# Attention and mixture-of-experts block: the causal mask inside the shift product, the rotation summed by VectorE out of a PSUM bank

## What is computed

```python
h = tok(x, channel_weights)                  # 12x224x224 image: 16x16 patches summed, 12 channels -> 192: 196 tokens
h = concatenate([h, txt], axis=1)            # + 32 text tokens: 228 tokens per batch item, 64 items
xn = norm_scale * layernorm(h) + norm_bias
q, k, v = split(xn @ W_attn + b_attn)        # 12 heads of 16
q, k = rope(q), rope(k)                      # o0 = x0*cos - x1*sin ; o1 = x0*sin + x1*cos
att = softmax([sink, causal(q @ k.T / 4)])[..., 1:]
h = h + (att @ v @ W_proj + b_proj) * rezero
h = h + moe(layernorm(h))                    # 8 experts, top 2, capacity 1.25, RMS norm, SwiGLU of width 512
```

## Time and profile before

| | us |
|---|---|
| median of three runs | 2927.87 (2925.61 to 2928.73) |
| the profiled execution | 2924.14 |
| its span | 2922.3 |
| TensorE busy | 2783.5 (95%) |
| TensorE weight loads busy | 2512.5 (86%) |
| VectorE busy | 2029.5 (69%) |
| GpSimd busy | 2019.7 (69%) |
| ScalarE busy | 1692.1 (58%) |
| mean granted TensorE clock | 0.979 of full |

### The profile page before, as it was taken

How to read it: one execution, slowest core, us unless ns; L and a number is a source line. 1 busy time by engine, 2 the same in 40 slices (tenths; PEclk the granted TensorE clock), 3 DMA queues, 4 the chain that set the end, 5 groups by cost and what they waited for, 6 DMA issues and landing times. The chain is left out here.

```text
span 2922.3 us, 65980 instructions
## 1 busy us (share of the span) xinstructions
PE 2783.5 (95%) x21712; PEld 2512.5 (86%) x21712; DVE 2029.5 (69%) x5657; ACT 1692.1 (58%) x4074; POOL 2019.7 (69%) x2070
## 2 busy tenths in 40 slices
PE   2899999999999999999999977999999999999998
PEld 1788888888888888888888866999999989999997
DVE  3577777777777777777777745767676767676766
ACT  0466666666666666666666644656565656565655
POOL 3578888888888888888888743656565655565665
PEclk8899999999999999999999978999999999999999
DMA  6455544444444444444344223333333333323242
GB/s 187 146 178 176 172 166 170 156 122 123 120 112 108 111 122 122 123 120 115 107 109 121 57 50 64 52 61 51 64 55 63 50 65 50 66 46 66 46 69 43
DMA packets 206006, 292.47 MB, mean 100 GB/s; under 512 B 95670, under 2 KB 167675, under 8 KB 205874
## 3 DMA queue, kind: packets, MB, share of 16 engines
q1 hardware_dynamic: 82642, 241.41, 28.1%
q0 software_dynamic: 122880, 47.00, 11.5%
q10 hardware_dynamic: 352, 2.41, 0.3%
HBM read 201.73 MB, written 93.90 MB: 101 GB/s over the span
## 5 line engine op out<-in xcount | busy, mean ns | idle before, releaser
L1494 POOL DMA_INDIRECT out<-arena,who x320 | 595.3, 1860 | 290.6 <-DVE who L1373 179.4
L572 DVE TENSOR_REDUCE top<-bank 114x2 f32<-114x456 f32 (+1 forms) x576 | 352.7, 622 | 85.9 <-PE bank L931 69.5
L687 POOL TENSOR_TENSOR arena<-arena 112x896 f32<-112x896 f32 x192 | 403.2, 2101 | 12.7 <-DMA arena<-in_x 12.7
L1467 PE MATMUL bank<-w_dn,hid 128*114 128x192 f32 x3840 | 401.9, 264 | 0.0
L1467 PEld LDWEIGHTS bank<-w_dn,hid 128*114 128x114 f32 x3840 | 390.3, 180 | 0.0
L1440 ACT ACTIVATE arena<-bank 128x456 f32<-128x456 f32 x320 | 176.2, 551 | 340.9 <-PE bank L1431 330.9
L1285 POOL DMA_INDIRECT moe_rows<-row,slot x256 | 293.8, 1148 | 102.8 <-issue 84.2
L549 ACT ACTIVATE pieces<-bank 64x456 fp32r<-64x456 f32 x384 | 209.2, 545 | 134.2 <-PE bank L907 131.9
L727 POOL TENSOR_TENSOR qk<-rot_c,qk 114x384 fp32r<-114x384 f32 x256 | 253.9, 1015 | 18.6 <-ACT qk L748 18.6
L1444 DVE TENSOR_TENSOR arena<-bank,arena 128x456 f32<-128x456 f32 x320 | 201.4, 630 | 93.7 <-ACT arena L1440 81.4
L1427 PE MATMUL bank<-pieces 128*128 128x456 f32 x640 | 240.1, 375 | 22.0 <-DVE arena L1444 15.4
(11 more groups left out here) (171 smaller groups left out, 7193.3 us busy)
## 6 DMA issues: line engine op xcount, KB each, us to landing
arena<-in_x SPq DMA_DIRECT2D x63, 2352.0 KB, 11.7
arena<-moe_rows SPq DMA_DIRECT2D x82, 363.4 KB
moe_rows<-filler SPq DMA_DIRECT2D x20, 1453.5 KB
out<-h SPq DMA_DIRECT2D x64, 171.0 KB
out<-arena,who POOLq DMA_INDIRECT x320, 5.0
arena<-in_w_t SPq DMA_DIRECT2D x9, 512.0 KB
arena<-in_w_t SPq DMA_DIRECT2D x18, 256.0 KB
moe_rows<-row,slot POOLq DMA_INDIRECT x256, 7.2
```

What stands on the lines that cost most here:

```text
L572: nc.vector.tensor_reduce(dst, src, AX.X, ALU.max).then_inc(maxed[k], 1)
L687: nc.gpsimd.tensor_tensor(xin[at.par][:, g, 0:mid], xin[at.par][:, g, 0:mid], xin[at.par][:, g, mid:XF], ALU.add).then_inc(x_folded, 1)
L1467: ins = nc.tensor.matmul(dst, hid2[:, j, h_part, at], w_dn2[e_par][:, j, w_part, :], start=(j == 0 and s % 2 == 0 and part == 0), stop=(j ...
L1494: nc.gpsimd.indirect_dma_start(out=out[:, :], out_offset=bass.IndirectOffsetOnAxis(ap=who[par][:, s:s + 1], axis=0), in_=ys[par][:, s, :], ...
```

## The change

The mask product of `score_t` goes. The selector has 14 live rows for shifts (heads are taken in two groups of six, so that two rows for each head of a group and two of ones are enough: `TOP` = 14), and its other 114 rows hold an identity; the matching rows of `shift_t` hold the mask, written once at the start. So one product brings shift and mask. `turn_shift` makes four transposes of 114x14 in place of two of 114x128; `round_shift` reads 456 columns for 228; `split_shift` is two instructions, 456 and 228 columns, for one of 228. The sine product is written back over the query and key bank, and VectorE makes the crosswise sum (with a wait on its own two products), so `rot_s` and GpSimd's `add_rotation` go. Bank 6 is free only after the sum: `make_qk(a, 1)` and `make_v` wait for `qk_rotated`, and `make_qk(a, 1)` stands after C4 instead of before it. Further: `sinks` are loaded twice, and set-up copies differ in shape.

```diff
@@ constants
-        sel[h, h] = -1
-        sel[HEADS + h, h] = -1
+        sel[h % PAIRS, h] = -1
+        sel[PAIRS + h % PAIRS, h] = -1
+        sel[TOP + q, h, q] = 1
+    low = np.zeros((128, 3, TT), f)
+    low[TOP:, 0] = low[TOP:, 2] = later.T
...
@@ rotate
                                     cos[:, t, :].unsqueeze(1).to_broadcast([TT, 48, 8]), ALU.mult)
-            nc.vector.tensor_tensor(rot_s[:, t, :].rearrange("p (a k) -> p a k", k=16), src.rearrange("p (a k) -> p a k", k=16),
-                                    sin[:, t, :].unsqueeze(1).to_broadcast([TT, 24, 16]), ALU.mult).then_inc(qk_read[t], 1)
+            nc.vector.tensor_tensor(src.rearrange("p (a k) -> p a k", k=16), src.rearrange("p (a k) -> p a k", k=16),
+                                    sin[:, t, :].unsqueeze(1).to_broadcast([TT, 24, 16]), ALU.mult).then_inc(qk_crossed, 1)
+            dve.wait_ge(qk_crossed, 4 * at.b + 2 * t + 2)
+            for half in range(2):
+                c, sn = (r.rearrange("p (a s k) -> p a s k", s=2, k=8)[:, :, i, :]
+                         for r, i in ((rot_c[:, t, :], half), (src, 1 - half)))
+                ins = nc.vector.tensor_tensor(c, c, sn, ALU.add)
+            ins.then_inc(qk_rotated[t], 1)
...
@@ split_shift
-            nc.vector.scalar_tensor_tensor(out=shift_t[:, :], in0=shift_hi[:, :].bitcast(fp32), scalar=split[:, 2:3],
-                                           in1=bank[7][:, 0:T], op0=ALU.mult, op1=ALU.add).then_inc(shift_ready, 1)
+            turned = bank[7][0:TOP, 0:4 * TT].rearrange("p (g t n) -> p g t n", g=2, t=2)
+            for to, of in ((slice(0, 2), slice(0, 2)), (slice(2, 3), slice(1, 2))):
+                ins = nc.vector.scalar_tensor_tensor(out=shift_t[0:TOP, :, to, :], in0=shift_hi[:, :, of, :].bitcast(fp32),
+                                                     scalar=split[0:TOP, 2:3], in1=turned[:, :, of, :], op0=ALU.mult, op1=ALU.add)
+            ins.then_inc(shift_ready, 1)
...
@@ make_qk, make_v
             if t == 1:
-                pe.wait_ge(qk_read[0], n)
+                pe.wait_ge(qk_rotated[0], n)
...
-            pe.wait_ge(qk_read[1], n)
+            pe.wait_ge(qk_rotated[1], n)
...
@@ turn_shift
-            for t in range(2):
-                ins = nc.tensor.transpose(bank[7][:, TT * t:TT * (t + 1)], shift[:, t, :], ident[0:TT, 0:TT])
+            for g in range(2):
+                for t in range(2):
+                    ins = nc.tensor.transpose(bank[7][0:TOP, TT * (2 * g + t):TT * (2 * g + t + 1)], shift[:, t, g, :],
+                                              ident[0:TT, 0:TT])
...
@@ score_t
                 for i in range(2):
-                    nc.tensor.matmul(dst[0:TT + 1, T * i:T * (i + 1)], sel[:, 2 * p + i, :], shift_t[:, :], start=False, stop=False)
-                ins = nc.tensor.matmul(dst[0:TT, 0:2 * T].rearrange("p (a n) -> p a n", a=2)[:, :, 0:TT], ident_r[0:TT, 0:TT],
-                                       mask_k[:, 0:2, :], start=False, stop=True)
+                    hh = 2 * p + i
+                    ins = nc.tensor.matmul(dst[0:TT + 1, T * i:T * (i + 1)], sel[:, hh, :],
+                                           shift_t[:, hh // PAIRS, 0:2, :].rearrange("p t n -> p (t n)"), start=False, stop=(i == 1))
             else:
-                nc.tensor.matmul(dst[0:TT, 0:4 * TT], ident_r[0:TT, 0:TT], mask_k[:, :, :], start=True, stop=False)
...
@@ step_tensor
             if z:
                 turn_xf(pe, z)
+            ring("C4")
             if a:
                 make_qk(pe, a, 1)
-            ring("C4 S5")
+            ring("S5")
...
@@ pass1_gpsimd
                     fold_image(pool, p, 1)
-                if a:
-                    add_rotation(pool, a, 0)
-                if p:
                     fold_image(pool, p, 2)
                 if a:
-                    add_rotation(pool, a, 1)
                     low_parts(pool, a, 0)
```

More of the change, by code:

```diff
@@ L28 @@
 PAIRS = HEADS // 2
+TOP = 2 * PAIRS + 2
 TXT = 32
@@ L67, in constants @@
     split[:, 1] = np.where(term >= 2, -1, 0)
-    split[HEADS:2 * HEADS, 2] = -1
-    split[2 * HEADS + 1, 3] = -1
+    split[PAIRS:2 * PAIRS, 2] = -1
+    split[2 * PAIRS + 1, 3] = -1
     small = np.zeros((128, 2 * E + 2), f)
@@ L84, in constants @@
         "mask_q0": np.ascontiguousarray(np.repeat(later[:, None], 4, 1)),
-        "mask_k": np.ascontiguousarray(np.repeat(later.T[:, None], 4, 1)),
+        "low": low,
         "sel": sel,
@@ L92, in constants @@
     }
-CONST_NAMES = ["cos", "sin", "ident", "mask_q0", "mask_k", "sel", "split", "small",
+CONST_NAMES = ["cos", "sin", "ident", "mask_q0", "low", "sel", "split", "small",
                "before", "patch", "filler"]
@@ L174, in build @@
         rez = sb("rez", [C1, 1])
-        sink_tok = sb("sink_tok", [TT, HEADS])
-        sink_top = bank[7][0:TT, 480:480 + HEADS]
+        sink_tok = sb("sink_tok", [TT, 2, HEADS])
+        sink_top = bank[7][0:TT, 480:480 + 2 * HEADS].rearrange("p (t a) -> p t a", t=2)
         sink_key = sb("sink_key", [128, HEADS])
@@ L210, in build @@
         top = sb("top", [TT, 2, HEADS])
-        shift = sb("shift", [TT, 2, 128])
-        shift_hi = sb("shift_hi", [128, T], fp32r)
-        shift_t = sb("shift_t", [128, T], fp32r)
+        shift = sb("shift", [TT, 2, 2, TOP])
+        shift_hi = sb("shift_hi", [TOP, 2, 2, TT], fp32r)
+        shift_t = sb("shift_t", [128, 2, 3, TT], fp32r)
         prob = sb("prob", [128, HEADS * T])
         staging, start = {}, 0
-        for name, rows, width in (("mask_q0", TT, 4 * TT), ("mask_k", TT, 4 * TT), ("sel", 128, HEADS * (TT + 1)),
+        for name, rows, width in (("mask_q0", TT, 4 * TT), ("low", 128, 3 * TT), ("sel", 128, HEADS * (TT + 1)),
                                   ("before", TT, TT), ("sink_col", 128, HEADS)):
@@ L309, in build @@
         v_made, v_ready = sem("v_made"), sem("v_ready")
-        qk_read = [sem(f"qk_read{t}") for t in range(2)]
+        qk_crossed = sem("qk_crossed")
         qk_rotated = [sem(f"qk_rotated{t}") for t in range(2)]
@@ L375, in setup_sync @@
                              .to_broadcast([GRP, SIDE * 2, D])).then_inc(loaded, 16)
-            for name in ("mask_q0", "mask_k", "sel", "before"):
+            for name in ("mask_q0", "low", "sel", "before"):
                 src = const[name]
@@ L438, in setup_vector @@
             for tile in (w_qkv[C:C1, :, :], pieces[:, 0:2 * QF].bitcast(fp32), k_t[0][:, :, :, TT:TT + 1].bitcast(fp32), k_t[1][:, :, :, TT:TT + 1].bitcast(fp32),
-                         shift[:, :, :], counts[0][:, :, :], counts[1][:, :, :], val[0][:, :, :, :], val[1][:, :, :, :], row[0][:, :, :],
+                         shift[:, :, :, :], counts[0][:, :, :], counts[1][:, :, :], val[0][:, :, :, :], val[1][:, :, :, :], row[0][:, :, :],
                          row[1][:, :, :]):
@@ L443, in setup_vector @@
             dve.wait_ge(step0, n)
-            for tile in (xn[:, :, :, C:C1], yn[:, :, :, C:C1], shift[:, :, 2 * HEADS:2 * HEADS + 2],
+            for tile in (xn[:, :, :, C:C1], yn[:, :, :, C:C1], shift[:, :, :, 2 * PAIRS:TOP],
                          val[0][:, :, :, HD:HD + 1], val[1][:, :, :, HD:HD + 1]):
@@ L447, in setup_vector @@
             dve.wait_ge(loaded, 16 * N_SMALL)
-            for dst, src in ((mask_q0[:, :, :], staging["mask_q0"]), (mask_k[:, :, :], staging["mask_k"]),
+            for dst, src in ((mask_q0[:, :, :], staging["mask_q0"]), (shift_t[:, 0, :, :], staging["low"]), (shift_t[:, 1, :, :], staging["low"]),
                              (sel[:, :, :], staging["sel"]), (before[:, :], staging["before"])):
```

40 lines of the change are left out of this document (18 added, 22 removed).

## The result

The changed kernel takes 2932.7 us (median of 20 runs, 2926.0 to 2941.3), the kernel before, in the same 20 rounds, 2926.5 (2923.6 to 2930.7). The ratio is 1.0023, with a 95% interval of 1.0015 to 1.0030: slower, by some 6 to 7 us (4 to 9 by the interval). The forecast was 2935 against 2927.9, a ratio of 1.0024. The profiled execution has a span of 2936.0 us.

A forecast was written before the change was run, and what follows sets the result against it. TensorE's own order was taken to set the pace until another engine is late. 3.42 + 8.40 + 13.82 = 25.64 us a step against 25.52, 60 times, is 7 us more: 2935 us, range 2900 to 2960.

The forecast's parts named there:

- A: Piece of a TensorE step from the first L863 (now L868) to the second; claimed 3.42 us, before 2.75.
- the own wait: VectorE's wait on its own sine product ahead of the two sums; claimed 0.04 us, at most 0.14.
- B: Piece of a TensorE step from the second L863 (now L868) to T0; claimed 8.40 us, before 8.69.
- the second branch: In B, from VectorE's L621 through ScalarE to GpSimd's low parts; claimed unshortened, ending at 8.36 us plus up to 0.14.
- T0: The point in a TensorE step at L907 (now L912) where B ends and C begins; claimed 8.4 us into B.
- C: Piece of a TensorE step from T0 to the next step's first L863; claimed 13.82 us, before 14.08.
- GpSimd's relief: GpSimd loses four sums in a step; claimed worth nothing, since what it hands over next waits for ScalarE's order.
- rival 1: TensorE keeps its pace: 1.09 us a step less, 65 us in all, 2863 us; chance 0.08.
- rival 2: VectorE's sums are cheap, 0.25 us each: step 25.22 us, 18 us less in all, 2910 us; chance 0.14.
- rival 3: VectorE's sums or sine product cost like a 384 column instruction: 0.94 us a step, 56 us more, 2984; chance 0.12.
- Rival 4: Weight loads pace TensorE, so a removed 456 column product gives what a 228 column one gives: 2941 us; chance 0.04.

The follow-up runs named there:

- e6: The changed kernel with rank moved behind S8 on TensorE; 2935.7 us.
- e7: e6 with ScalarE's high parts of half 1 also moved ahead of exp_gap and exponential 6; 2905.0 us.
- e2: The kernel before with only the new rotation (VectorE's sums in the bank, second L863 behind C4), mask as before; 2950.9 us.
- e1: The changed kernel with the rotation and its place in the orders undone, so the new mask alone; 2899.9 us.
- e3: The changed kernel with the sine product in SBUF and the bank freed after the two products, sums still on VectorE; 3406.9 us.
- e12: e10 with GpSimd's three folds each one place earlier and VectorE's weigh moved behind normalize; 3108.8 us.
- e10: e1 with the two moves of e7; 2885.0 us.
- e9: e7 with VectorE's seven small operations of weigh moved behind normalize; 2911.2 us.

## Why the prediction was right, and where it was not

**Right, step by step.** A was to be 3.42 and is 3.41, held by VectorE's sums (0.350 us each, forecast 0.355; the pair 0.62, forecast 0.63; sine into its own bank 0.56, forecast 0.55; 0.03 for the own wait, forecast 0.04). B was to be 8.40 and is 8.35: L634 starts 4.23 behind the second L868 (forecast 4.29), rank 5.77 (forecast 5.84), and the second branch ends at T0 too, which e6 and e7 showed by taking away one and then both. C was to be 13.82: 13.83 in the step above, 13.90 in the median. The step is 0.14 longer against a forecast 0.12, and 60 x 0.14 = 8 us stand beside 6 to 7 measured. e2 shows that the rotation alone costs 25 us and e1 that the mask alone gives 28, so the small result is a difference of two larger ones, as the sum had it. GpSimd's relief is worth nothing in the changed kernel (its waits for ScalarE in L731 are 146 us), as forecast.

**Rivals.** TensorE does not keep its pace (rival 1); it waits at the two places named. The sums are neither cheap (rival 2) nor dear (rival 3): 350 ns. Rival 4 fails in the rows. (e1's time alone does not settle it: its interval takes in the 20 us that the same rival gave for e1.) An S item with a 456 column mask product (L960, L962, L965) takes 0.83 us ahead of L920 before the change, and without it (L968, L973) 0.62 ahead of L925, each the median of 43 steps. So the removed product gave its whole 0.21, not 0.11.

**Sizes that were off.** The wait ahead of L1049 was to be 0.73; the row says 0.43. Most of this is how a wait is counted: L936 before it starts at 1018.76 and is worth 0.11, so TensorE could have gone on at 1018.87 and went on at 1019.47, 0.60 later. The row counts from the modelled end, 1019.03. The other 0.13 is 0.06 of TensorE being later than I had it (the first product behind L868 takes 0.5 whichever it is: L968 0.52 now, L929 0.51 before, so C4 was worth a little less there) and 0.07 of VectorE being earlier. Likewise at the second L868: 0.40 in the row, 0.56 from start to start. The four transposes take 0.39, that is 0.14 more than two where I took 0.20; and L1012, released 7.11 behind T0 (forecast 7.23), loses 0.08 to 0.25 again in the 0.40 to 0.57 until L961. Against these two stands 0.10 that nobody had counted, a hidden wait of the kernel before that went away (next paragraph). They cancel in C to within 0.08, and that is luck.

**What the prediction did not see.** It said that a removed matmul gives its full time until another engine is late, and that by the waits none was. In A VectorE was exactly in time already, with a hidden wait of 0.2 for it. For the changed kernel this made no difference, since A is VectorE's sum in any case; it made e1 slower than expected. In C there was a second one, at `turn_shift` (L940 before, L946 after). It stands 0.22 us behind the last transpose of T0 to T2 in the kernel before and 0.11 in the changed kernel and in e2. On VectorE before:

```profile
1023.79 0.20 DVE L579 TENSOR_TENSOR shift<-top,bank 114x48 f32<-114x48 f32 x1
```

It ends at 1023.99 and L940 starts at 1024.05: 0.06 behind it in every step, as in e1 and e7, where `make_shift` holds TensorE too; in the changed kernel and in e2 TensorE comes 0.15 to 0.25 behind it. This is 0.10 of the 0.12 by which C is shorter in e2 than before. The prediction also took "GpSimd loses four sums" as worth nothing without asking what GpSimd's work does to VectorE: it is only because the sine product stays in the bank that VectorE can take the sums at all (e3).

**Open.** Whether the loop's branch is what costs 0.17 in every second step; what moving the high parts without moving rank would give.

## What to carry to other kernels

Before you remove work from an engine, walk every chain that leaves it and comes back, and take the slack from start to start of the rows, not from the list of waits: a wait of 0.2 us can be missing there. Where two branches end at one point, shortening one gives nothing (e6; e7, with both, took 31 us less). Price a move to VectorE by what GpSimd does at that moment and by where the operands lie, and look at the granted clock behind each new wait of TensorE: in e12 a wait of 1.3 us came with 3.5 to 5.0 us more in a step.

## What was not expected of the hardware

- VectorE's sum of 192 columns takes 344 to 356 ns with an operand in PSUM, whatever GpSimd does; with both in SBUF it takes up to 2240 ns beside GpSimd's tensor operations (e3).
- A tensor_scalar on two columns in SBUF, 0.16 us elsewhere, took 2.56 until the end of a fold of GpSimd that had started after it (e12). Beside GpSimd's indirect DMA instructions another of weigh's (114 x 2 too) takes 442 ns in the mean in e10 and 479 in the changed kernel, where it takes 169 in e9.
- Waits of TensorE of 1.3 us in a step that is else busy were followed by a granted clock of 0.54 (e12); waits of 0.4, two in each step, left it at 1.00 over 1100 us (the changed kernel).
